# Routing a mixture of experts by a slot-to-row map instead of an indirect scatter (graph network and experts, one core)

## The reference

```python
x = x + _L1_gnn_ref(_layernorm(x), edge_index, weight, bias)      # mean over edges, projection, row norm
x = x + _L1_ffn_ref(_layernorm(x)[None], gate_w, gate_b, w1, b1, w2, b2)[0]

def _L1_ffn_ref(h, ...):               # E = 8 experts, C = ceil(1.25 * 12500 / 8) = 1954 places each
    probs = softmax(x @ gate_w + gate_b); idx = argmax(probs); prb = max(probs)
    pos = (cumsum(one_hot(idx)) * one_hot(idx)).sum(-1) - 1        # place in the queue of its expert
    kept = pos < C
    buf = zeros((E, C, D)).at[idx, where(kept, pos, C)].set(x, mode='drop')
    ybuf = relu(buf @ w1 + b1) @ w2 + b2
    return nan_to_num(ybuf[idx, minimum(pos, C - 1)] * (prb * kept))
```

## Time and profile before

| what | value |
|---|---|
| median of 3 runs | 6364.5 us (6361.77 to 6368.09) |
| the profiled execution's own time | 6367.77 us |
| its span, first to last instruction | 6365.9 us |
| mean granted TensorE clock | 0.886 of 2.4 GHz |
| busy over the span | PE 78%, PEld 70%, DVE 62%, ACT 28%, POOL 65% |
| q0, the software queue (POOL's) | 183392 packets, 501.66 MB |
| q1, a hardware queue (SP's loads and stores among it) | 424972 packets, 334.16 MB |

### The profile page before, as it was taken

The page is one execution under the profiler, slowest core; times in us unless marked ns, Lnnn a source line. Parts: engine busy times, 40 slices in busy tenths (PEclk is TensorE's granted clock), DMA queues, the critical chain, the costliest instruction groups (busy, mean ns, idle before and its releaser), DMA issues. The chain is left out here.

```text
span 6365.9 us, 102080 instructions
## 1 busy us (share of the span) xinstructions
PE 4966.5 (78%) x33831; PEld 4443.7 (70%) x33832; DVE 3976.5 (62%) x9818; ACT 1755.5 (28%) x4052; POOL 4158.5 (65%) x4039
## 2 busy tenths in 40 slices
PE   4427999999999999999985666666666666665887
PEld 3326999999999999999984554454545544554887
DVE  6526898888888898888863333333333433334776
ACT  2202444444444444444440000000000000002554
POOL 1347777777777777777727777777777777771111
PEclk9658999999999999999997877787777777777999
DMA  6555555656555655666524444444444444443221
GB/s 189 154 153 148 164 164 160 163 163 167 158 161 166 165 164 160 163 164 165 159 76 129 127 136 128 127 128 134 126 123 122 126 120 118 119 120 106 69 79 50
DMA packets 639158, 877.60 MB, mean 138 GB/s; under 512 B 254782, under 2 KB 447376, under 8 KB 638050
## 3 DMA queue, kind: packets, MB, share of 16 engines
q0 software_dynamic: 183392, 501.66, 27.0%
q1 hardware_dynamic: 424972, 334.16, 19.4%
q10 hardware_dynamic: 30326, 35.87, 1.7%
HBM read 766.70 MB, written 155.49 MB: 145 GB/s over the span
## 5 line engine op out<-in xcount | busy, mean ns | idle before, releaser
L1241 POOL DMA_INDIRECT m_ring<-tab_a,m_src x1764 | 1994.1, 1130 | 675.1 <-issue 501.7
L1859 POOL DMA_INDIRECT eb_rows<-tab_b,eb_src x1764 | 1712.5, 971 | 541.1 <-issue 537.1
L2100 PE MATMUL eb_acc<-eb_rows,eb_S 128*128 128x257 f32 x3528 | 1133.2, 492 | 511.2 <-DMA eb_rows<-tab_b,eb_src 509.8
L2100 PEld LDWEIGHTS eb_acc<-eb_rows,eb_S 128*128 128x128 f32 x3528 | 886.4, 256 | 719.1 <-DMA eb_rows<-tab_b,eb_src 534.6
L1522 PE MATMUL m_acc<-m_V,m_S 128*128 128x264 f32 x3528 | 864.7, 391 | 0.0
L1926 DVE TENSOR_TENSOR eb_sum<-eb_acc,eb_sum 128x257 f32<-128x257 f32 x98 | 41.8, 426 | 1238.4 <-PE eb_acc L2100 1238.4
L1522 PEld LDWEIGHTS m_acc<-m_V,m_S 128*128 128x128 f32 x3528 | 648.9, 192 | 94.2
L1643 ACT ACTIVATE mh_high<-m_ps,bn_b,bn_s 128x256 fp32r<-128x256 f32 x784 | 441.3, 563 | 755.7 <-PE m_ps L534 752.5
L522 DVE TENSOR_TENSOR mh_low<-mh_full,mh_high 128x512 fp32r<-128x512 f32 x784 | 544.2, 694 | 109.5 <-ACT mh_full L1643 75.2
L1632 ACT ACTIVATE mh_full<-m_ps,bn_b,bn_s 128x256 f32<-128x256 f32 x784 | 400.5, 563 | 665.3 <-DVE mh_low L522 346.7
L1316 DVE TENSOR_TENSOR m_V<-m_ring,m_V 128x1280 f32<-128x1280 f32 (+1 forms) x392 | 532.8, 1359 | 13.4
(11 more groups left out here) (372 smaller groups left out, 10305.1 us busy)
## 6 DMA issues: line engine op xcount, KB each, us to landing
m_dstb<-dst_p SPq DMA_DIRECT2D x196, 320.0 KB
m_dstb<-dst_p SPq DMA_DIRECT2D x196, 256.0 KB
buf<-empty SPq DMA_DIRECT2D x49, 771.0 KB
m_ring<-tab_a,m_src POOLq DMA_INDIRECT x1764
eb_rows<-tab_b,eb_src POOLq DMA_INDIRECT x1764, 2.8
xw_stage<-in_L_ffn_w_dram ACTq DMA_DIRECT2D x16, 1024.0 KB, 8.2
over<-b_blank SPq DMA_DIRECT2D x9, 1452.0 KB, 15.3
mOV<-over SPq DMA_DIRECT2D x49, 264.0 KB, 4.8
```

Of the source, the lines that this page charges most:

```text
L1241: gp.indirect_dma_start(out=ring[:, j, :], out_offset=None, in_=scratch["tab_a"], in_offset=bass.IndirectOffsetOnAxis(ap=src[:, j:j + 1], ...
L1859: gp.indirect_dma_start(out=rows_[q.par][j][:, t, 0:D], out_offset=None, in_=scratch["tab_b"], in_offset=bass.IndirectOffsetOnAxis(ap=src_ ...
L2100: last_i = nc.tensor.matmul(ps_acc[j][:, 0:NR], S[q.par][j][:, t, :], rows_[q.par][j][:, t, :], start=t == 0, stop=t == WT - 1)
```

## The change

Rows are no longer scattered to their slots. ACT writes the rows of a group to a DRAM tensor `routed` in their own order, with a plain DMA, once the probability is in. The slot of each token is split into a high part (slot / 128) and a low part; VectorE writes both as 0/1 rows in bf16, the high one twice, times the token's lane and times its tile number plus 1; TensorE adds up their products over all 98 tiles in one PSUM bank (`record`). At the end of mean_route this gives, for each slot, the row number: `row_of` (0 for an empty slot) and `out_of` (FAR or more, or negative, for an empty one). In experts POOL gathers the 256 rows of a chunk by two indirect DMAs, of 513 values a row, into `XG` (`fetch`, in the order fetch, send within a chunk); TensorE turns from XG, ACT copies the other 257 values to `XB` (`keep`). The fills of `buf`, `empty` with its three writes, and the column `tok` are gone. VectorE waits for the landing of the sends itself.

```diff
@@ bounds, attend_mix (SP)
-            sp.wait_ge(blank_ok, 2)
-                for lo, hi, of in ((0, D, blank[:, 0:D]), (D, 2 * D + 1, blank[:, 0:D + 1]), (2 * D + 1, XW, far[:, :])):
-                    sp.dma_start(scratch["empty"][:, lo:hi], of).then_inc(blanked, 16)
+            sp.wait_ge(blank_ok, 1)
...
-                    if e == 6:
-                        sp.dma_start(scratch["buf"][bass.ds(q.n * (FILL * P), FILL * P), :].rearrange("(t p) f -> p t f", p=P),
-                                     scratch["empty"].rearrange("p (x f) -> p x f", x=1).to_broadcast([P, FILL, XW])).then_inc(filled, 16)
@@ mean_route (POOL)
-            def scatter(q):
-                gp.wait_ge(slot_ok, q.n + 1)
-                for j in pair:
-                    gp.indirect_dma_start(out=scratch["buf"], out_offset=bass.IndirectOffsetOnAxis(ap=slot_i[q.par][:, j:j + 1], axis=0),
-                                          in_=XR[q.par][:, j, :], in_offset=None,
-                                          bounds_check=NX * SLOTS - 1, oob_is_err=False).then_inc(sent[q.par], 16)
...
-                if has(q, 2):
-                    scatter(q.prev().prev())
                 gather(q, 1)
             groups(gp, body)
-            scatter(end.prev())
-            scatter(end)
@@ mean_route (VectorE), finish
-                v.wait_ge(x_out[p], q.half * 16 + 16)
                 if has(q, 2):
-                    v.wait_ge(sent[p], q.half * 32)
+                    v.wait_ge(x_out[p], q.half * 32)
...
-                nc.vector.tensor_scalar(tok[:, :], tok[:, :], float(2 * P), None, ADD).then_inc(tok_ok, 1)
-                step(nc.vector.tensor_copy(XR[p][:, :, 2 * D + 1:XW].rearrange("p t x -> p (t x)"), tok[:, :]))
...
-                nc.vector.scalar_tensor_tensor(slot_i[p][:, :], first[:, :], float(SLOTS), pos[:, :], MUL, ADD).then_inc(slot_ok, 1)
+                step(nc.vector.scalar_tensor_tensor(slot[:, :], first[:, :], float(SLOTS), pos[:, :], MUL, ADD))
+
+                step(nc.vector.tensor_scalar(hi_i[:, :], slot[:, :], 1.0 / P, 0.5 / P - 0.5, MUL, ADD))
+                step(nc.vector.tensor_copy(hi[:, :], hi_i[:, :]))
+                step(nc.vector.scalar_tensor_tensor(lo[:, :], hi[:, :], -float(P), slot[:, :], MUL, ADD))
+                if has(q, 1):
+                    v.wait_ge(map_ps, n)
+                for j in pair:
+                    nc.vector.tensor_scalar(low_hot[:, j, :], k["iota"][:, :], lo[:, j:j + 1], None, ALU.is_equal).then_inc(hot_ok, 1)
+                    nc.vector.tensor_scalar(high_hot[:, j, 0, :], k["iota"][:, :], hi[:, j:j + 1], lane[:, 0:1], ALU.is_equal, MUL)\
+                        .then_inc(hot_ok, 1)
+                    nc.vector.tensor_scalar(high_hot[:, j, 1, :], k["iota"][:, :], hi[:, j:j + 1], float(2 * n + j + 1), ALU.is_equal, MUL)\
+                        .then_inc(hot_ok, 1)
@@ mean_route (VectorE), after the last group
+            v.wait_ge(map_ps, Q)
+            nc.vector.tensor_scalar(tokens[:, :], ps_m[:, HI:2 * HI], float(P), -float(P), MUL, ADD).then_inc(tot_ok, 1)
+            nc.vector.tensor_scalar(blank_slot[:, :], ps_m[:, HI:2 * HI], 0.0, float(FAR), ALU.is_equal, MUL).then_inc(tot_ok, 1)
+            v.wait_ge(tot_ok, 5)
+            nc.vector.tensor_tensor(tokens[:, :], tokens[:, :], ps_m[:, 0:HI], ADD).then_inc(tot_ok, 1)
+            v.wait_ge(tot_ok, 6)
+            nc.vector.tensor_scalar(k["row_of"][:, :], tokens[:, :], 0.0, None, MAX).then_inc(tot_ok, 1)
+            nc.vector.tensor_tensor(k["out_of"][:, :], tokens[:, :], blank_slot[:, :], ADD).then_inc(tot_ok, 1)
@@ mean_route (TensorE); record(q.prev()) stands behind sum_up(q, 1, 1)
+            def record(q):
+                pe.wait_ge(hot_ok, q.n * 6 + 6)
+                for j in pair:
+                    last_i = nc.tensor.matmul(ps_m[:, 0:2 * HI], low_hot[:, j, :], high_hot[:, j, :, :].rearrange("p x h -> p (x h)"),
+                                              start=q.n + j == 0, stop=last(q) and j == 1)
+                last_i.then_inc(map_ps, 1)
@@ mean_route (ACT), end of a group
+                s.wait_ge(oh_ok, q.n + 1)
+                s.dma_start(rows(scratch["routed"], q), XR[q.par][:, :, :]).then_inc(x_out[q.par], 16)
@@ experts (SP): the loads of XN and XB
-            def chunk(g, row, e, par, first):
-                sp.wait_ge(T_ok, g + 1)
-                sp.dma_start(XN[:, :, :], rows(row)[:, :, 0:D]).then_inc(n_in, 16)
-                sp.wait_ge(r_free, g + 1)
-                sp.wait_ge(r_in, g * 16 + 16)
-                sp.dma_start(XB[:, bass.ds(g % 2, 1), :, :].rearrange("p x t f -> p (x t) f"), rows(row)[:, :, D:XW]).then_inc(r_in, 16)
@@ experts (POOL)
+            def fetch(g, column):
+
+                gp.wait_ge(T_ok, g + 1)
+                hold(gp, passed)
+                gp.wait_ge(r_in, g + 1)
+                hold(gp, passed)
+                gp.tensor_copy(of_row[:, :], k["row_of"][:, bass.ds(column, CT)]).then_inc(of_ok, 1)
+                gp.wait_ge(of_ok, g + 1)
+                hold(gp, passed)
+                for j in range(CT):
+                    gp.indirect_dma_start(out=XG[:, j, :], out_offset=None, in_=scratch["routed"],
+                                          in_offset=bass.IndirectOffsetOnAxis(ap=of_row[:, j:j + 1], axis=0)).then_inc(fetched, 16)
+
+            def send(g):
                 gp.wait_ge(row_ok, g + 1)
...
-                gp.wait_ge(sent, g * (16 * CT) + 16 * CT)
-                gp.sem_inc(row_free, 1)
+            def chunk(g, column, e, par, first):
+                fetch(g, column)
+                send(g)
@@ experts (VectorE), last step of finish, and in chunk ahead of turned_low
-                v.wait_ge(row_free, g + 1)
-                step(nc.vector.tensor_copy(tok[:, :], xb(D + 1, D + 2).rearrange("p t f -> p (t f)")))
+                v.wait_ge(sent, g * (16 * CT) + 16 * CT)
+                v.wait_ge(out_ok, g + 1)
+                step(nc.vector.tensor_copy(tok[:, :], of_out[:, :]))
...
+                nc.vector.tensor_copy(of_out[:, :], k["out_of"][:, bass.ds(column, CT)]).then_inc(out_ok, 1)
                 turned_low(g + 2)
@@ experts (TensorE), turn
-                pe.wait_ge(n_in, loaded)
+                pe.wait_ge(fetched, loaded)
@@ experts (ACT), behind turned_high of each chunk
+            def keep(c):
+                s.wait_ge(fetched, c * (16 * CT) + 16 * CT)
+                s.wait_ge(r_free, c + 1)
+                hold(s, passed)
+                nc.scalar.copy(XB[:, bass.ds(c % 2, 1), :, :].rearrange("p x t f -> p (x t) f"), XG[:, :, D:XW]).then_inc(r_in, 1)
```

More of the change, by code:

```diff
@@ L133, in build @@
             phase(attend_mix, a, k, scratch)
+        k["row_of"] = sbuf(top, "row_of", [P, HI], I32)
+        k["out_of"] = sbuf(top, "out_of", [P, HI])
         phase(mean_route, a, k, scratch, out)
@@ L1733, in mean_route @@
     before_ = [small(f"before{i}", NX, BF16) for i in pair]
-    slot_i = [small(f"slot_i{i}", 2, I32) for i in pair]
+    slot, hi, lo = map(small, ("slot", "slot_hi", "slot_lo"))
+    hi_i = small("slot_hi_i", 2, I32)
+    low_hot = sbuf(ctx, "low_hot", [P, 2, P], BF16)
+    high_hot = sbuf(ctx, "high_hot", [P, 2, 2, HI], BF16)
+    tokens, blank_slot = (sbuf(ctx, n, [P, HI]) for n in ("slot_tokens", "slot_blank"))
     xT = sbuf(ctx, "rxT", [P, 2, D])
@@ L1753, in mean_route @@
     x_out = [s_(f"x_out{i}") for i in pair]
[L1754 to L1757, removed]
+    w_in, const, lane_ok, ss_ok, x3_ok, hot_ok, map_ps = map(s_, ("w_in", "const", "lane_ok", "ss_ok", "x3_ok", "hot_ok", "map_ps"))
+    o_ok, xl_ok, T_ok, xT_ok, lg_ps, le_in, le_ok, oh_ok, cum_ps = map(s_, (
+        "o_ok", "xl_ok", "T_ok", "xT_ok", "lg_ps", "le_in", "le_ok", "oh_ok", "cum_ps"))
     G_ok, TG_ok, GT_ok = map(s_, ("G_ok", "TG_ok", "GT_ok"))
@@ L2160, in body @@
                 sum_up(q, 1, 1)
+                if has(q, 1):
+                    record(q.prev())
             groups(pe, body)
@@ L2171, in _ @@
         def _(s):
-            for i in pair:
-                first_turn(s, k, x_out[i])
             def body(q):
@@ L2315, in chunk @@
                                           bounds_check=N - 1, oob_is_err=False).then_inc(sent, 16)
-                gp.wait_ge(sent, g * (16 * CT) + 16 * CT)
-                gp.sem_inc(row_free, 1)
+            def chunk(g, column, e, par, first):
+                fetch(g, column)
+                send(g)
             done = all_experts(gp, "x_pool", nothing, chunk, nothing)
-            chunk(gp.snap(done, min_val=1, max_val=MOST), None, None, None, False)
+            g = gp.snap(done, min_val=1, max_val=MOST)
+            fetch(g, 0)
+            send(g)
+            send(g + 1)
+            gp.wait_ge(sent, g * (16 * CT) + 2 * 16 * CT)
         @block.vector
@@ L2447, in chunk @@
                 pe.sem_inc(y_ps, 1)
-            turn(16)
+            turn(32)
             all_experts(pe, "x_pe", before, chunk, nothing)
@@ L2473, in _ @@
             turned_high(2)
```

(2 more changed lines are left out.)

86 lines of the change are left out of this document (40 added, 46 removed).

## The result

The changed kernel takes 6248.8 us (6242.7 to 6251.0), the kernel before 6366.3 us beside it on the same chip (6361.8 to 6369.9): a ratio of 0.981, 95% interval 0.980 to 0.982, or -117.5 us. That is faster by 1.9%, as forecast, and inside the range; the forecast was -102. The profiled execution of the changed kernel has a span of 6249.3 us against 6365.9, -116.6, and can be cut at the same events in both traces.

The account below looks back on a forecast made before the run. POOL's instruction stream was taken to set mean_route's length, with TensorE nearest to full in experts. The terms -124 + 5 - 1 - 1 + 11 + 8 = -102 us took 6364.5 to 6262 us, range 6228 to 6305.

Parts of the forecast that it names:

- Scatters, -124: mean_route: 94 in-loop scatters leave POOL's queue at 1.31 us each (quiet stretch), -124 us; 149 with the longer wholes.
- One-hots, +5: mean_route: VectorE's one-hots beside POOL's gathers stretch them by 0.1 us a group, +5 us; ends 0 and 66.
- The bound of 66: mean_route: upper end of the one-hot term, 1.36 us x 49 groups if all six held POOL in full.
- Routed write, attend_mix, ACT's keep: 0: Plain write moved to ACT in mean_route, 49 fills gone from attend_mix, ACT's copy in experts: 0 us each.
- bounds, -1: bounds: three small writes on SP go, at most 0.65 us of issue each, -1 us.
- End of mean_route, -1: mean_route's end: 4.1 us of map work against 3.06 of issue and a 3.7 landing; -1 us, between -3 and +2.
- Copy of out_of, +11: experts, VectorE: two-column copy between YR and xxT_low counts in full, 37 chunks x 0.3 = +11 us, 7 to 18.
- Late gathers, +8: experts, POOL: gathers queued behind two sends land 0.2 us late on the mean, 37 x 0.2 = +8 us.
- Fetch late: Rival, experts: POOL's fetch instructions, held by VectorE, come 1.2 us late a chunk; 44 instead of 8, 6298 us; 15%.
- One-hots hold POOL: Rival, mean_route: one-hots hold POOL back, +66 instead of +5 us, 6323 us; 6%.
- removal frees nothing: Rival, mean_route: 0.305 us is the DMA ring's pace, remaining gathers stretch, only costs stay: +22, 6386 us; 2%.
- A landing of 8.5 us: Slower rival, experts: gathers always land as late as the slowest load, turns wait 4.6 us, +60, 6424 us; 3%.

## Why the prediction was right, step by step

- **Scatters, -124.** Right: -122 between the first and the last gather. The choice of 94 x 1.31 over 94 x 1.58 rested on the comparison staying and meeting a gather instead; the run with two small DMAs a group shows just that, 26 us changing hands. That the cost is POOL's time for each instruction, with bytes playing no part, is shown by the same run.
- **One-hots, +5.** The bound of 66 fell: doubled, they cost nothing that shows. The 0.1 us a group is too small to be told from the runs' own 10 us.
- **Routed write, attend_mix, ACT's keep: 0.** Right for the fills, shown; no wait for the other two stands out in the trace after, which is no test of its own.
- **bounds, -1.** Not to be told: the first gather of mean_route lay between 3342.4 and 3346.2 in the runs that leave the earlier stages as the change made them, with the writes put back at 3345.3.
- **End of mean_route, -1.** The step that failed: "4.1 us [...] against 3.06 of issue and the 3.7 of a landing". The new work was sized well (slot ready 5657.36, map ready 5661.90: 4.5 us). (By its own numbers the sum is 4.1 - 3.06 - 3.7 = -2.7; it took -1 and gave no reason.) What it was set against was too short: the 11.6 us between the last landing (5784.08 + 2.3 us) and the experts' start were taken as a fixed cost of the stage's end, while 8.2 us of them were POOL's drain, which costs only when POOL arrives last. Without it 7.9 us went behind the ready slots. The gap was in the rows read, and no step asked what filled it. The end of the span holds such a drain too, priced at nothing: -2.9 us.
- **Copy of out_of, +11.** Too much: "so it counts in full" added the copy's 0.3 us to a pause of 0.22 us that VectorE made there anyway. The copy starts in that pause and xxT_low does not wait for it: it comes 0.08 us later in the chunk shown. And the step before it failed too: "This is on the chain that ends TensorE's wait" read the earlier trace rows as a wait for xxT_low, where at most boundaries TensorE's wait for its own last product ended later. The pause grew by 0.02 us a chunk on the median, under 1 us in all.
- **Late gathers, +8.** The mechanism was right, the size 10 to 13: about 0.3 us a chunk instead of 0.2. The working came out near (second gather at +5.64, +5.55 reckoned); the gathers take 1.06 us on the mean, some 1.3 to 1.5, where 0.98 was used. That the experts came out near the forecast, +15.9 against +19, is luck: the copy was priced some 10 us too high, the gathers 2 to 5 too low, the shorter drain and the later first turn were not priced, and a few us stay untraced.
- **The rivals.** *Fetch late*, 1.2 us a chunk: in part, a quarter of that. By the rule of the Trainium skill that it was set beside (SBUF — State Buffer, "Who interferes with whom") POOL's reads contend with two-input VectorE instructions; the mean of 1.25 us for the small DMAs that overlap the large comparison, against 0.94 for those that don't, agrees with it, while in the experts the sends went from 984 to 1015 ns and the gathers took 1057, on the mean under 0.1 us each of the 0.5 that the rival assumed. *One-hots hold POOL* and *removal frees nothing* are out by a run each. *A landing of 8.5 us* always didn't come up: the gathers' median is 3.6 us, and the longest, 7.9, is one of the experts' first two.

## What to carry to other kernels

An instruction queue that runs without a gap is worth its length, whatever its instructions move: 94 indirect DMAs with 32 bytes a row cost 116 us where 94 with 2056 had cost 122. A stage's end is a step of its own: look at what each engine does between its last instruction and the next stage's first, and let the one with the longest way out arrive first. The end of attend_mix is still such a place: SP's drain there was done at 3334.3 us and POOL's, the last, at 3337.1 in the changed kernel. An addition to a chain costs only what goes beyond the pauses already there. The profile names one wait where two run side by side, and taking one away shows the other.

## What was not expected of the hardware

- POOL needs 9.65 us from its last wait to the next stage, VectorE 3.55 us from its last operation. The difference is POOL's first drain behind indirect DMAs, 5.94 us there and 8.23 in the kernel before, though the DMAs had landed; a second drain takes 0.04 us, so that one taken early hides it (3.75 us). What it does in that time was not tried. The Trainium skill (GPSIMD Engine Reference, "Instruction dispatch") states that the first call of freshly loaded code on this engine costs about 6 us with no visible instruction. The size is near that of one of these drains, but the trace does show an instruction, the drains took from 3.49 to 8.23 us, and no run here shows that code was loaded.
- An indirect DMA that stands at VectorE's 128x1152 comparison took up to 1.80 us with 32 bytes a row and up to 2.04 us with 2056 (the earlier trace rows has one of 2.01); away from it none of these took over 0.95 and 1.15 us.
